# One transpose for a batch's row maxima, and turned scores that wait for each of two query operations on its own

## What is computed

```python
q = q.reshape(B, N, 16, 16); k = ...; v = ...
scores = einsum('bqhd,bkhd->bhqk', q, k) * scale     # scale = 16 ** -0.5
w = softmax(scores, axis=-1)                          # subtracts each row's maximum
out = einsum('bhqk,bkhd->bqhd', w, v)
```

## Time and profile before

| | |
|---|---|
| median of 3 runs | 1671.42 us (1670.57 to 1672.57) |
| profiled execution, its own time | 1671.03 us |
| span of that execution in the trace | 1669.2 us |
| PE busy | 1501.2 us, 90% |
| DVE busy | 1096.9 us, 66% |
| ACT busy | 943.5 us, 57% |
| POOL busy | 719.1 us, 43% |
| mean granted TensorE clock | 0.972 of full speed |

### The profile page before, as it was taken

How to read it: one execution, slowest core, us unless ns; L and a number is a source line. 1 busy time by engine, 2 the same in 40 slices (tenths; PEclk the granted TensorE clock), 3 DMA queues, 4 the chain that set the end, 5 groups by cost and what they waited for, 6 DMA issues and landing times.

```text
span 1669.2 us, 44764 instructions
## 1 busy us (share of the span) xinstructions
PE 1501.2 (90%) x17760; PEld 1305.8 (78%) x17760; DVE 1096.9 (66%) x2373; ACT 943.5 (57%) x1722; POOL 719.1 (43%) x982
## 2 busy tenths in 40 slices
PE   4979999999999999999998989989899898989987
PEld 3868878787887878788786787878788787887866
DVE  4556766666766666667776766766767666676654
ACT  3456565556656565666645645556565555645543
POOL 3133424334242433335646445464554636455411
PEclk9899999999999999999998989999999999999988
DMA  6110100101010010100112000000000000000000
GB/s 211 47 47 10 45 16 15 52 13 55 10 46 15 15 53 13 55 27 27 33 45 65 11 17 15 14 27 11 17 15 14 26 12 17 18 24 2 2 14 14
DMA packets 34251, 49.39 MB, mean 30 GB/s; under 512 B 3488, under 2 KB 24928, under 8 KB 34048
## 3 DMA queue, kind: packets, MB, share of 16 engines
q1 hardware_dynamic: 34048, 46.54, 9.0%
HBM read 38.07 MB, written 8.45 MB: 28 GB/s over the span
## 4 chain that ended last, share of the span: by engine, by line
PE 67%; DVE 15%; issue 8%; ACT 8%; POOL 1%; DMA 0%; SPq 0%; DVEq 0%; ACTq 0%; POOLq 0%
PE score_t L670 8%; PE score L652 7%; PE p_unit L546 6%; PE p_unit L739 5%; PE p_mix L712 5%; PE p_unit L548 5%; PE p_unit L547 5%; DVE neg_max L1108 3%; PE p_out L548 3%; PE p_out L547 3%; PE p_out L546 3%; PE p_out L701 2%; PE p_mix L577 2%; PE score_t L546 2%; PE score_t L548 2%
## 5 line engine op out<-in xcount | busy, mean ns | idle before, releaser
L1108 DVE TENSOR_REDUCE neg_max<-score 128x8 f32<-128x1024 f32 x224 | 273.9, 1223 | 150.0 <-PE score L652 141.3
L652 PE MATMUL score<-k_t,q_t 32*128 32x256 f32 x1792 | 264.7, 413 | 54.1 <-DVE q_less L1118 28.7
L670 PE MATMUL score_t<-q_less,k_t 32*128 32x128 f32 x3584 | 273.4, 293 | 11.5 <-ACT probs_t L970 6.2
L670 PEld LDWEIGHTS score_t<-q_less,k_t 32*128 32x128 f32 x3584 | 229.8, 195 | 23.3 <-issue 14.9
L652 PEld LDWEIGHTS score<-k_t,q_t 32*128 32x128 f32 x1792 | 167.7, 194 | 94.8 <-issue 38.0
L972 ACT ACTIVATE probs_t<-score_t 128x1024 f32<-128x1024 f32 x168 | 172.0, 1024 | 113.4 <-PE score_t L670 100.7
L892 ACT ACTIVATE xt<-p_mix,mod_now 128x128 f32<-128x128 f32 x384 | 154.3, 454 | 94.3 <-PE p_mix L577 66.5
L1311 POOL TENSOR_TENSOR xt_lo<-xt,xt_hi 128x256 fp32r<-128x256 f32 x128 | 94.6, 739 | 243.1 <-ACT xt_hi L897 242.2
L739 PE MATMUL p_unit<-w_out,heads_t 128*128 128x256 f32 x512 | 144.9, 406 | 18.8 <-ACT q_t L936 8.2
L1156 DVE TENSOR_TENSOR hid_lo<-hid,hid_hi 128x256 fp32r<-128x256 f32 x256 | 145.2, 567 | 8.8
L546 PE MATMUL p_out<-w_hi,hid_lo 128*128 128x256 f32 x512 | 147.4, 288 | 0.8 <-issue 0.8
(11 more groups left out here) (158 smaller groups left out, 4264.1 us busy)
## 6 DMA issues: line engine op xcount, KB each, us to landing
ctxt<-in_ctxT SPq DMA_DIRECT2D x16, 512.0 KB, 3.8
side<-gates SPq DMA_DIRECT2D x15, 512.0 KB, 5.5
x_new<-in_x SPq DMA_DIRECT2D x32, 128.0 KB, 2.0
x_mid<-xs SPq DMA_DIRECT2D x8, 512.0 KB, 3.4
x_new<-x_mid SPq DMA_DIRECT2D x32, 128.0 KB, 2.0
out<-xs SPq DMA_DIRECT2D x8, 512.0 KB, 2.9
k_t<-in_L_f_wT SPq DMA_DIRECT2D x2, 1024.0 KB, 5.7
probs_t<-in_L_xcond_fc_w SPq DMA_DIRECT2D x1, 1024.0 KB, 11.2
```

What stands on the lines that cost most here:

```text
L652: mm = pe.matmul(score_banks(b, h)[:, r % 2, t * 2 * N:(t + 1) * 2 * N].rearrange("p (e n) -> p e n", e=2), q_t[s][rows(r), t, tokens], k_ ...
L670: mm = pe.matmul(turned_banks(b, h)[:, r % 2, x * N:(x + 1) * N], k_t[s][rows(r), t, e, tokens], q_less[rows(r), j % 2, t, e, :], start=Tr ...
L1108: dve.tensor_reduce(by_half[:, 2 * h:2 * h + 2, :, :, 0], score_banks(b, h)[:].rearrange("p r (t e n) -> p r t e n", t=CT, e=2), AX.X, ALU ...
```

## The change

The change has three parts, which need each other in the data layout.

- `neg_max` becomes one tile of 128 columns: the maximum of head (r, t, e) is in column 32r + 16e + t. `turn_max` is one transpose, not two. `less_max` reads the same 128 transposed columns for both t (a broadcast), and picks rows with `head_mask` where it picked them with `one_row`. The row of ones in the keys is now row t of its 16, so that each t picks its own maximum.
- Since that row differs between t = 0 and 1, the bias does too: `low_keys` and `high_keys` become two instructions of 256 columns each, where they were one of 512, and a preparation on DVE becomes four instructions, where it was two.
- `queries_less` becomes two semaphores, one for each DVE instruction. A round waits for the first at its head, and `turned_scores` goes through its parts as t0 e0, t1 e0, t0 e1, t1 e1; ahead of the third part of a batch's first half it waits for the second semaphore. All other waits on `queries_less` take the second.

No stage is moved to another step.

```diff
-        one_row = sb("one_row", [P, 2])
+        one_row = sb("one_row", [P, 2, CT])
...
-        neg_max = sb("neg_max", [P, 2, CT, P])
+        neg_max = sb("neg_max", [P, 2, P])
...
             def turned_scores(group, s, b, h):
                 j = 4 * s + b
-                pe.wait_ge(queries_less, group * 8 + j + 1)
+                pe.wait_ge(queries_less[0], group * 8 + j + 1)
...
-                def products(x):
-                    t, e = divmod(x, 2)
+                def products(part):
+                    e, t = divmod(part, CT)
+                    x = 2 * t + e
+                    if part == CT and h == 0:
+                        pe.wait_ge(queries_less[1], group * 8 + j + 1)
                     for r in (2 * h, 2 * h + 1):
                         mm = pe.matmul(turned_banks(b, h)[:, r % 2, x * N:(x + 1) * N], k_t[s][rows(r), t, e, tokens],
                                        q_less[rows(r), j % 2, t, e, :], start=True, stop=True)
-                    if x == SLOTS - 1:
+                    if part == SLOTS - 1:
                         mm.then_inc(scored_t, 1)
...
             def turn_max(group, j):
...
-                for t in range(CT):
-                    mm = pe.transpose(p_out[:, t * P:(t + 1) * P], neg_max[:, j % 2, t, :], ident[:])
-                mm.then_inc(max_turned, 1)
+                pe.transpose(p_out[:, 0:P], neg_max[:, j % 2, :], ident[:]).then_inc(max_turned, 1)
...
             def low_keys(group, unit):
...
-                act.activation(k_t[s][:, :, 0, half * HALF:(half + 1) * HALF],
-                               rot[:, 0, :].rearrange("p (t n) -> p t n", t=CT),
-                               ACT.Identity, scale=head_mask[:, 0:1], bias=one_row[:, 0:1]).then_inc(keys_low, 1)
+                for t in range(CT):
+                    op = act.activation(k_t[s][:, t, 0, half * HALF:(half + 1) * HALF], rot[:, 0, t * HALF:(t + 1) * HALF],
+                                        ACT.Identity, scale=head_mask[:, 0:1], bias=one_row[:, 0, t:t + 1])
+                op.then_inc(keys_low, 1)
...
             def high_keys(group, unit):
...
-                dve.tensor_scalar(k_t[s][:, :, 1, half * HALF:(half + 1) * HALF],
-                                  rot[:, 0, :].rearrange("p (t n) -> p t n", t=CT),
-                                  head_mask[:, 1:2], one_row[:, 1:2], ALU.mult, ALU.add).then_inc(keys_high, 1)
+                for t in range(CT):
+                    op = dve.tensor_scalar(k_t[s][:, t, 1, half * HALF:(half + 1) * HALF], rot[:, 0, t * HALF:(t + 1) * HALF],
+                                           head_mask[:, 1:2], one_row[:, 1, t:t + 1], ALU.mult, ALU.add)
+                op.then_inc(keys_high, 1)
...
-                by_half = neg_max[:, j % 2].rearrange("p t (r e w) -> p r t e w", e=2, w=HD)
-                dve.tensor_reduce(by_half[:, 2 * h:2 * h + 2, :, :, 0],
+                by_half = neg_max[:, j % 2].rearrange("p (r e w) -> p r w e", e=2, w=HD)
+                dve.tensor_reduce(by_half[:, 2 * h:2 * h + 2, 0:CT, :],
...
                 for e in range(2):
-                    op = dve.scalar_tensor_tensor(q_less[:, j % 2, :, e, :],
-                                                  p_out[:, 0:CT * N].rearrange("p (t n) -> p t n", t=CT),
-                                                  one_row[:, e:e + 1], q_t[s][:, :, b * N:(b + 1) * N],
-                                                  ALU.mult, ALU.add)
-                op.then_inc(queries_less, 1)
+                    dve.scalar_tensor_tensor(q_less[:, j % 2, :, e, :],
+                                             p_out[:, 0:N].unsqueeze(1).broadcast_to([P, CT, N]),
+                                             head_mask[:, 1 - e:2 - e], q_t[s][:, :, b * N:(b + 1) * N],
+                                             ALU.mult, ALU.add).then_inc(queries_less[e], 1)
```

More of the change, by code:

```diff
@@ L350, in build_blocks @@
         max_turned = sem("max_turned")
-        queries_less = sem("queries_less")
+        queries_less = [sem(f"queries_less{e}") for e in range(2)]
         scored_t = sem("scored_t")
@@ L433, in _ @@
                 (head_mask[:], a["head_mask"]),
-                (one_row[:], a["one_row"]),
+                (one_row[:].rearrange("p e t -> p (e t)"), a["one_row"]),
                 (bias_cols[:], a["bias_cols"]),
@@ L693, in turn_max @@
                 if group or j:
-                    pe.wait_ge(queries_less, group * 8 + j)
+                    pe.wait_ge(queries_less[1], group * 8 + j)
                 if j == 4:
@@ L765, in down @@
                 if u == 0:
-                    pe.wait_ge(queries_less, (group + 1) * 8 + (4 if group < GROUPS - 1 else 0))
+                    pe.wait_ge(queries_less[1], (group + 1) * 8 + (4 if group < GROUPS - 1 else 0))
                 if u == 0 and group == 0:
@@ L792, in body @@
                     elif t == MOD_LN_AT:
-                        pe.wait_ge(queries_less, 4)
+                        pe.wait_ge(queries_less[1], 4)
                         modulation_ln()
@@ L916, in move_unit @@
                     elif kind == "q":
-                        act.wait_ge(queries_less, last)
+                        act.wait_ge(queries_less[1], last)
                     else:
@@ L1271, in _ @@
             for e in range(2):
-                dve.tensor_scalar(key_bias[:, e], bias_cols[:, 0:4], head_mask[:, e:e + 1], one_row[:, e:e + 1],
-                                  ALU.mult, ALU.add).then_inc(ready, 1)
+                for t in range(CT):
+                    dve.tensor_scalar(key_bias[:, e].rearrange("p (s t) -> p t s", t=CT)[:, t],
+                                      bias_cols[:, 0:4].rearrange("p (s t) -> p t s", t=CT)[:, t],
+                                      head_mask[:, e:e + 1], one_row[:, e, t:t + 1], ALU.mult, ALU.add).then_inc(ready, 1)
             dve.tensor_scalar(mask_all[:], mask_cols_u8[:], MASKED, None, ALU.mult).then_inc(ready, 1)
             dve.tensor_copy(bias_v_wide, bias_v[:].unsqueeze(3).broadcast_to([P, 2, CT, P])).then_inc(bias_spread, 1)
-            dve.wait_ge(ready, 14)
+            dve.wait_ge(ready, 16)
             def modulation(layer, k, full, src, bias, n):
@@ L1464 @@
         "bias_v": np.concatenate([cols(qkv_b[2][by_slot]), cols(kv_b[1][by_slot])], axis=1),
-        "one_row": (row[:, None] % 32 == np.array([0, HD])).astype(np.float32),
+        "one_row": (row[:, None] % 32 == np.array([0, 1, HD, HD + 1])).astype(np.float32),
         "mask_cols": get["mask_BxS2_bf0"].reshape(B, N).astype(np.uint8).T,
```

## The result

The changed kernel takes 1654.62 us (median of 4 runs, 1654.12 to 1659.33), the kernel before 1670.99 beside it (1670.35 to 1672.57). The ratio is 0.991, with a 95% interval from 0.9896 to 0.9925. That is 16.4 us less by the medians and 15.0 by the ratio, which goes by the means of the runs. The forecast was 1654. The profiled execution took 1654.51 us, with a span of 1652.7 and a mean granted clock of 0.974 (before: 0.972).

A forecast was written before the change was run, and what follows sets the result against it. The prediction took the kernel to be bound by PE's in-order queue, with short detours over DVE and ACT. Terms -9.7 - 12.8 + 3.4 = -19.1 us from 1671.4 gave 1652.3; with 1.7 taken back, 1654 us, range 1643 to 1665.

The forecast's parts named there:

- One transpose fewer, -9.7: PE's transposes of the maxima: one fewer per group of maxima, 88 counted on the chain at 0.11 us, 9.7 us less.
- Waiting for the first operation alone, -12.8: PE's score rounds resume 0.39 us sooner at 26 waits for q_less, plus 2.7 us from j = 1 stalls; 12.8 less.
- Keys in pairs, +3.4: Layer 1 key operations as pairs: 0.22 us more on ACT, 0.20 on DVE, once each in 8 groups; 3.4 more.
- what I took back: 1.7 us, a tenth of the summed saving, deducted for places where a saving ends in one of the other waits.
- Savings coming back by half (1662): Rival: with PE earlier, detours over ACT and DVE are late next and half the saving returns; 1662 us, chance 0.16.
- a second wait that stalls (1665): Rival: the second query wait, inside the round, stalls where the first did, losing the 12.8 us; 1665 us, chance 0.07.
- The satisfied wait that costs (1678): Rival: the mid-round wait stops weight loads running ahead, up to 0.20 us at each of 128; 1678 us, chance 0.07.
- The clock (1629): Rival: shorter PE waits in layer 1 keep the clock at 2.4 GHz, 24.5 us more saved; about 1629 us, chance 0.07.

The follow-up runs named there:

- filled kernel: Changed kernel plus identity products, six and four, in PE's two long waits of each layer-1 group; 1636.73 us, ratio 0.9804.

## Why the prediction was right

**One transpose fewer, -9.7.** Right in the whole, wrong as a part by itself. In the changed kernel the six transposes of a layer-0 group give 0.65 (1.17 less the split's 0.52), for 6 x 0.11 = 0.66. Without the split they give 0.48, and the run without it shows -6.9 for the term. The step that failed is that I took "on the chain" for "counts in full", in what I expected of that run. I had excluded j = 4 of layer 1 because the round behind it waits for DVE, and the same reason holds for j = 1 in both layers, a stall that stands in my own rows. Some of the transposes' saving also ended at the wait for the heads, which is 10.4 us with the transposes fewer and 8.8 without, with the split or not.

**Waiting for the first operation alone, -12.8.** Right in kind, 2.2 too large by the medians: -10.6 alone, with 12.8 still inside the interval (7.5 to 13.2). In layer 0 it gives 0.33 from j = 5 to 7 for the 0.39 priced, and 0.19 at j = 1 for 0.17. I had forecast 26 waits with some 18 us in sum; there are 17 with 19.8. The waits near 0.39 vanish from the list, and a longer one like that of the earlier trace rows shrinks by 0.29 only, as PE comes to it 0.10 earlier. The second wait cost nothing: the third part kept its distance of 0.55, and 640 more waits changed nothing.

**The extra that I had left out.** By the medians it is -3.4: -10.6 - 6.9 + 4.5 = -13.0, and the change gives -16.4. I had written that the shorter transpose doesn't help where the round is held. That is so before the split. Where the split removes the whole stall it does help, and this interaction was no term of my sum. The rows show 0.07 to 0.09 of it at j = 1, in each of 16 groups, so some 1.2 to 1.4 us; layer 0 as a whole shows 8 x 0.17 = 1.4. The rest is within the uncertainty of the times, and stays open.

**Keys in pairs, +3.4.** The term was a little small: +4.5, interval 3.0 to 6.7, so 3.4 is still inside it. ACT's pair cost 0.27 a group at the copy of the heads, for 0.22 priced, and the stretch with both pairs 0.49 for 0.42. The durations held (1.08 and 0.72 us a pair for 1.02 and 0.73), but for one that I did not foresee, below.

The Trainium skill (VectorE: DVE Perf Modes, The TRN2 errata), which spoke against this part, gave an estimated 2.0. The measured term is over twice that, and its whole interval lies above it; the direction agrees.

**The sum and what I took back.** -19.1 in all, less 1.7 for savings that end in other waits, so -17.4. The measurement gives -16.4. Some savings did end there: the wait for the heads grew by 1.6 us. The wait for the copy of the heads grew by 2.2, but that is ACT's key pair and no lost saving, as it grew the same with the pairs alone. By the profiled executions the two layers are unlike. Seven whole groups of layer 0 gave 8.6 us together (676.96 to 668.37), 1.23 each for a forecast of 1.2. The 64 batches of layer 1, from the first transpose to the last, gave 5.2 (811.31 to 806.10), 0.65 a group for the forecast 1.1, at the same mean clock of 0.96. The start up to the second group gave 2.9, and there kernels that all contain the change differ by up to 3 us among themselves. So layer 0 was forecast rightly, and layer 1 too high, 8.6 for 5.2.

**How much of it was luck.** The mechanism and layer 0 were right. That the time came within 1 us of the forecast was luck in part: the parts measured one by one add to -13.0 and not -19.1, layer 1 gave less than its terms; an interaction that I had no term for, the deduction of a round tenth and an uneven start made up the difference.

**The rivals.** Savings coming back by half (1662) and a second wait that stalls (1665) are out, by the time and by the rows. The satisfied wait that costs (1678) is out by its own experiment. The clock (1629) wasn't triggered by this change, as 1.64 and 1.22 us of idleness stayed: the mean is 0.974 for 0.972. But as a mechanism it was real, and as large as the change itself. Filling the two waits gave 17.9 us, for the 24.5 that I had priced at 3.1 for each of eight groups.

The Trainium skill (TensorE: Matmul & The Clock Gate, What's actually happening) says that activity lifts the clock. The filled kernel agrees, with 1.00 in the groups where the change alone has 0.97, though its products compute nothing of use.

## What to carry to other kernels

Before counting a saving that stands ahead of a wait, look whether that wait is held by another engine. At j = 1 the shorter transpose gave 0.01 of its 0.11 us alone and 0.08 once the other side was shortened too, so such edits should be tried together. A consumer that waits for the last of two operations, and needs only the first to begin, can be given two semaphores; the satisfied wait was free here. And where the clock falls behind two short waits in a row, price the clock before the waits: 2.6 us of products with no use in each group bought about as much as all the savings of the change.

## What the hardware showed that I had not expected

**One key operation of 1.51 us, for 0.40.** In six of the eight layer-1 groups the second operation of one DVE pair takes 1.51 us; in the other two the first takes 1.35 and the second 0.81. Timelines of DVE and POOL in the changed kernel:

```profile
1115.81 1.90 DVE L1101 TENSOR_SCALAR k_t<-side,head_mask,one_row 128x256 f32<-128x256 f32 x2
...
1118.99 1.23 DVE L1111 TENSOR_REDUCE neg_max<-score 128x8 f32<-128x1024 f32 x1
...
1116.27 1.29 POOL L1368 TENSOR_TENSOR q_t<-q_t,side 128x512 f32<-128x512 f32 x1
```

The same place in the kernel before:

```profile
1130.72 0.60 DVE L1098 TENSOR_SCALAR k_t<-side,head_mask,one_row 128x512 f32<-128x512 f32 x1
...
1133.86 1.23 DVE L1108 TENSOR_REDUCE neg_max<-score 128x8 f32<-128x1024 f32 x1 [1.25 <-PE score L652]
...
1131.18 1.30 POOL L1364 TENSOR_TENSOR q_t<-q_t,side 128x512 f32<-128x512 f32 x1
```

Before, the one operation was under way when POOL's third rotation began, and took 0.60. Now the second of the pair begins with POOL's operation (its row starts 0.07 us earlier) and ends at 1117.72, just behind POOL's end at 1117.56. So the split of the keys costs 1.3 us of DVE here and not 0.20. It costs little time, since DVE had 1.25 us of slack before the next `row_max`, and that slack is now gone: the row at 1118.99 has no idle time before it. But the next round of PE needs these keys, and the chain of the changed kernel goes through them:

```profile
1115.81 1.91 DVE k_t L1101 x2
...
1117.82 0.39 PE score L652
```

That round starts 0.39 us behind the last product of the unit ahead of it, where it was 0.35, and the stretch from j = 0 to 1 grew from 9.78 to 9.82: the price is 0.04 a group. The next saving on PE at this place would give nothing.

The Trainium skill (SBUF — State Buffer, SBUF: two separate sides) says that GpSimd and certain DVE operations, those in a two-port mode or with two SBUF inputs, share a port pair, and that the one that comes second "fully blocks" until the other's instruction is done. The durations agree with that: in the changed kernel and in the one with key pairs alone, the six operations of 1.51 us in each end 0.15 us behind the end of this POOL operation. The kernel before has such an operation too, of 1.48, in the first two groups of layer 1 alone. The order doesn't show, as DVE's row starts first. No run here moved the POOL operation away, so the cause is read from the rows and not shown.

**Satisfied waits.** 768 of them between products of 32 rows left the time where it was: 1655.51 us with them and 1654.62 with 128.
